# Adapter attention: the second chunk's mask is prepared two steps sooner

## The chip, the cores and the metric

The program runs on one core of one Trainium2 chip. The metric is the device time of one execution in microseconds (us), as the median of three. The engines named below are TensorE (PE, the matrix unit; PEld is its weight load), VectorE (DVE), ScalarE (ACT), GpSimd (POOL) and SyncE (SP), which here only issues DMAs.

## The reference, cut to what matters

A post-norm decoder layer over 16 sequences of 128 rows, width 256. Three blocks follow one another: self attention (16 heads of 16), adapter attention (32 heads of 8, with a mask, plus a second attention over a context tensor), and a block with attention of 16 heads of 128 and a mixture of four experts.

```python
x = _layernorm(x + _L0_attn_ref(x, L0_attn_Wqkv, ...), axis=-1)
x = _layernorm(x + _L0_xattn_ref(x, mask_Bx1xSxS_fk0, ctx_2048, L0_xattn_Wq, ...), axis=-1)
x = _layernorm(x + _L0_ffn_ref(x, ...), axis=-1)

# _L0_xattn_ref, the block that the change touches
scores = jnp.einsum('bhqd,bhkd->bhqk', q, k) * inv_sqrt_d
scores = scores + attention_mask
scores = jnp.maximum(scores, jnp.finfo(scores.dtype).min)
w = jax.nn.softmax(scores.astype(jnp.float32), axis=-1)
attn_output = jnp.einsum('bhqk,bhkd->bhqd', w, v)
# plus tanh(gate) * softmax(q a_k) a_v with keys and values from ctx_2048
```

The mask is a float tensor of [16, 1, 128, 128], one 128x128 block for each sequence.

## The kernel before

The first two attention blocks (A, the self attention, and B, the adapter attention) share one software pipeline. It is a loop over steps s from -20 to 361, and every engine runs its own copy of the loop with its own list of what it does at each step. Semaphores tie the engines together; the order of the instructions on each engine is fixed by the step tables alone. All of A's units (4 heads of one sequence, n = 0 to 63) and B's units (n = 64 to 319, in pairs from step 64) go through three passes: `pass1` (scores, whose row maxima the DVE takes), `pass2` (the same scores turned, with the maxima subtracted by extra rows of the stack), `pv` (the product with the values). For B, `pass2` of a unit comes 26 steps after `pass1`, and `pv` 30 steps after it.

The sequences of B come in chunks of two: chunk c = 8 is the first of B, c = 9 the second, whose units start at step 96 (unit 96). A chunk of B has 32 steps. `bg0(c)` is the step to which the background work of a chunk is tied: 44 for c = 8, 64 for c = 9, then 32 more for each. `places` makes tables {step: (chunk, k)} from offsets to `bg0`: `xts` (turning of the inputs), `projs` (projections, with `evacs`, `ropes`, `sums`, `splits`, `parts` and `stacked` derived from them), `masked` and `vals` (values).

How a chunk's mask becomes usable. The mask [128, 2, 128] lies in `MK`. The mask has to be added inside PE by a matmul with bf16 operands, so it is split into three bf16 parts:

- `clamp` (DVE, line 800), at the step in `clamps`
- `mask_part` and `mask_rest` in turn, at the steps in `mask_parts`: ACT line 1042, POOL line 1175, ACT line 1045, POOL line 1177. They write the tile `B_MQ`.
- `mask_out` (SP, DMA `Bmask<-B_MQ`), at `masks_out`, and two steps later `mask_rows` (SP, DMA `B_MP<-Bmask`), which reads it back in another layout. `mask1` on PE (line 562, matmuls `bank<-B_MP,B_pick`) adds it to the scores of `pass1`; the chunk's first unit needs it, at step 96 for c = 9.
- `masks` (PE, line 536) turns the f32 mask at `masked`, ACT (line 1005) copies it out of PSUM into `MT` one step later. `mask_parts_turned` (PE, line 545) turns the three parts at `mask_turns`, ACT (line 1011) copies them into `B_MTQ`, and SP sends them out and back at `masks_t_out` (`Bmask<-B_MTQ`, `B_MTP<-Bmask`) for `pass2`, which is 26 steps later.

Of one step, PE does `pv`, the mask products, `pass2` and `pass1` first. From step 87 on values and the small turns follow, then `transpose_in`, projections, `masks` and `mask_parts_turned`; before step 87 the values and small turns stand behind these. Each small PE product gets its PSUM bank from the table `home`, which deals banks 5, 6, 7 in rotation up to step 85 and banks 6, 7 from step 86 in the order of the steps; `turn` on PE waits until the bank's user before it has been read.

What SP does in these steps, in this order within a step: load of the mask (`load_mask`), `shift` (rows `B_nmT` that carry the maxima into the stack), `stack_in` (six DMAs `stk<-Bdrq`, `stk<-Bdrk` or `stk<-Bdra` each, from DRAM into the stack of q, k or adapter k), `mask_out`, `mask_rows`, `mask_t_out`, `mask_t_rows`, `parts_out` (two DMAs `Bdrk<-PB` and so on). All run through one queue on SP, in order: a DMA that waits holds up every one behind it. `shift(17)`, at step 101, feeds `pass2` of units 80 and 81 at step 106.

Of the kernel before, what the change touches and what calls it, by code (L numbers as in the profile page):

```python
# [43 lines left out]
def program(nc, I, out):  # L44
# [204 lines left out]
    def bg0(c):  # L249
        return 8 * c - AHEAD if c < 9 else NA + 32 * (c - 9)  # L250

    def places(A, B8, B9, B):

        return {max(bg0(c) + r, -AHEAD): (c, k) for c in range(16)
                for k, r in enumerate(A if c < 8 else B8 if c == 8 else B9 if c == 9 else B)}

    xts = places((-1,), (-2, -4), (-2, 4), (-8, 8))
    projs = places((2, 6), (2, 6, 10), (0, 10, 13), (-4, 9, 13))
    masked = places((), (11,), (23,), (18,))
    clamps = {s - (6 if c < 10 else 7): c for s, (c, _) in masked.items()}  # L260
    mask_parts = [{s + k: c for s, c in clamps.items()} for k in (1, 2, 3, 4)]
    masks_out = {s + 5: c for s, c in clamps.items()}
# [2258 lines left out]
```

## Time and profile before

| | us |
|---|---|
| median of three runs | 1181.89 (1181.88 to 1181.89) |
| profiled execution, its own time | 1185.99 |
| its span | 1184.2 |
| PE busy | 1116.1 (94%) |
| PE weight load busy | 921.1 (78%) |
| DVE busy | 954.0 (81%) |
| ACT busy | 667.3 (56%) |
| POOL busy | 660.2 (56%) |

The profiled execution is 4.1 us longer than the median, and its span 1.8 us shorter than its own time. The step tables place the second chunk's mask work between about 209 and 231 us of the span. Blocks A and B end near 550 us; the rest is the third block, which the change does not touch.

How to read the rows: a timeline row gives start, duration, engine, line, operation, `out<-in`, shape and count; in brackets is the idle time of the engine before it, and what ended it. Several instructions of one form that follow each other stand in one row. `SPq` is a DMA being issued, not the transfer. PEclk 1.00 is TensorE's clock of 2.4 GHz, 0.50 is 1.2 GHz.

### The profile page before, as it was taken

How to read it: one execution, taken by the hardware profiler on the slowest of the kernel's cores; microseconds unless marked ns; L12 is line 12 of the kernel's file. 1: busy time of each engine (PE TensorE's matmuls, PEld its weight loads, DVE VectorE, ACT ScalarE, POOL GpSimd, SP SyncE). 2: the span in 40 equal slices, each digit the busy share in tenths (PEclk: the TensorE clock that was granted, in tenths of full speed). 3: DMA queues.
4: the chain of work that ended last, by engine and by line, in shares of the span. 5: the costliest groups of instructions: out<-in, count | busy, mean ns of one | idle time of the engine just before them, and what ended most of it. 6: DMA issues, size and time to landing. Idle time of an engine off the chain costs nothing.

```text
span 1184.2 us, 30629 instructions
## 1 busy us (share of the span) xinstructions
PE 1116.1 (94%) x11732; PEld 921.1 (78%) x11732; DVE 954.0 (81%) x2219; ACT 667.3 (56%) x1703; POOL 660.2 (56%) x714
## 2 busy tenths in 40 slices
PE   6899999899999999888999999999999999999997
PEld 5667665566666766556899899999999899988887
DVE  6758886877888878867788888888898888878977
ACT  5466564577777777664555544444444444558663
POOL 4457564654545556264778554544544455737665
PEclk9889999989999999989999999999999999999999
DMA  5975544344444444402121000000000100101111
GB/s 162 211 183 131 130 122 110 99 122 120 120 135 135 117 126 119 121 22 86 58 72 55 2 1 1 1 1 1 1 1 1 37 2 1 37 19 36 37 37 36
DMA packets 107490, 83.05 MB, mean 70 GB/s; under 512 B 74171, under 2 KB 95803, under 8 KB 107345
## 3 DMA queue, kind: packets, MB, share of 16 engines
q1 hardware_dynamic: 107345, 81.10, 25.0%
q8 instruction: 93, 1.52, 0.5%
q14 instruction: 52, 0.43, 0.1%
HBM read 57.02 MB, written 23.07 MB: 68 GB/s over the span
## 4 chain that ended last, share of the span: by engine, by line
PE 55%; DVE 14%; issue 6%; POOL 4%; ACT 2%; SPq 1%; DMA 1%; POOLq 0%; DVEq 0%; ACTq 0%
PE bank L1637 5%; PE bank L1638 5%; PE bank L1639 5%; PE bank L1693 4%; PE bank L1666 4%; PE bank L665 3%; PE bank L643 3%; PE bank L562 3%; PE bank L1653 2%; PE bank L1708 2%; PE bank L1706 2%; PE bank L1707 2%; DVE B_nr L808 2%; PE bank L1654 2%; PE bank L1655 2%
## 5 line engine op out<-in xcount | busy, mean ns | idle before, releaser
L1941 POOL TENSOR_TENSOR C_QK<-C_t1b,C_t2b 128x512 f32<-128x512 f32 x128 | 168.7, 1318 | 227.4 <-DVE C_t2b L1780 226.8
L1777 DVE SCALAR_TENSOR_TENSOR C_t1b<-bank,C_bcol,C_tabs 64x512 f32<-64x512 f32 x256 | 192.1, 750 | 38.6 <-PE bank L1639 34.5
L1067 ACT ACTIVATE PT<-bank 128x512 f32<-128x512 f32 x224 | 130.0, 596 | 98.5 <-PE bank L643 96.7
L808 DVE TENSOR_REDUCE B_nr<-bank 128x4 f32<-128x512 f32 x256 | 164.2, 683 | 25.4 <-PE bank L604 25.1
L1637 PE MATMUL bank<-C_XTh,C_Wh 128*128 128x512 f32 x256 | 112.4, 439 | 5.7 <-DVE C_XTl L1626 1.9
L1873 ACT ACTIVATE C_P<-bank,C_nm 128x128 f32<-128x128 f32 x256 | 90.5, 366 | 34.1 <-DVE C_nm L1790 32.4
L1892 ACT ACTIVATE C_V<-bank 128x512 f32<-128x512 f32 x64 | 38.0, 596 | 124.1 <-PE bank L1655 122.6
L1638 PE MATMUL bank<-C_XTl,C_Wh 128*128 128x512 f32 x256 | 101.6, 397 | 0.0
L1639 PE MATMUL bank<-C_XTh,C_Wl 128*128 128x512 f32 x256 | 101.2, 395 | 0.0
L665 PE MATMUL bank<-PT,vpool 128*32 128x128 f32 x2048 | 97.6, 287 | 2.0 <-ACT OTf L1077 2.0
L1780 DVE SCALAR_TENSOR_TENSOR C_t2b<-bank,C_bcol,C_tabs 128x512 f32<-128x512 f32 x128 | 96.1, 751 | 1.8
L643 PEld LDWEIGHTS bank<-stk 54*128 54x128 bf16 (+1 forms) x1280 | 49.4, 96 | 50.6 <-issue 37.3
L1881 ACT ACTIVATE C_OTh<-bank,C_bcol 128x512 fp32r<-128x512 f32 x64 | 44.1, 689 | 73.7 <-PE bank L1693 73.1
L604 PE MATMUL bank<-stk 48*128 48x128 bf16 (+1 forms) x1280 | 77.0, 220 | 6.2 <-DVE B_nr L808 5.9
L643 PE MATMUL bank<-stk 54*128 54x128 bf16 (+1 forms) x1280 | 77.2, 222 | 3.9 <-DMA stk<-A_nmT 3.5
L1801 DVE SCALAR_TENSOR_TENSOR C_OTl<-bank,C_bcol,C_OTh 128x512 fp32r<-128x512 f32 x64 | 47.9, 748 | 38.8 <-ACT C_OTh L1881 38.7
L1653 PE MATMUL bank<-C_Wh,C_XTh 128*128 128x256 f32 x256 | 72.5, 283 | 1.6 <-DVE C_t2b L1780 1.3
L1706 PE MATMUL bank<-C_Wh,C_OTh 128*128 128x256 f32 x256 | 71.9, 281 | 0.4 <-DVE C_OTl L1801 0.4
L1654 PE MATMUL bank<-C_Wl,C_XTh 128*128 128x256 f32 x256 | 71.9, 281 | 0.0
L1655 PE MATMUL bank<-C_Wh,C_XTl 128*128 128x256 f32 x256 | 71.9, 281 | 0.0
L1708 PE MATMUL bank<-C_Wh,C_OTl 128*128 128x256 f32 x256 | 71.7, 280 | 0.0
L1707 PE MATMUL bank<-C_Wl,C_OTh 128*128 128x256 f32 x256 | 71.6, 280 | 0.0
(271 smaller groups left out, 3495.0 us busy)
## 6 DMA issues: line engine op xcount, KB each, us to landing
Adrq<-PB SPq DMA_DIRECT2D x16, 192.0 KB, 2.9
Adrk<-PB SPq DMA_DIRECT2D x16, 192.0 KB, 3.1
stk<-Adrq SPq DMA_DIRECT2D x16, 192.0 KB
stk<-Adrk SPq DMA_DIRECT2D x16, 192.0 KB
Bdrq<-PB SPq DMA_DIRECT2D x16, 192.0 KB, 3.0
stk<-Bdrq SPq DMA_DIRECT2D x32, 96.0 KB
Bdrk<-PB SPq DMA_DIRECT2D x16, 192.0 KB, 2.8
stk<-Bdrk SPq DMA_DIRECT2D x32, 96.0 KB
```

The costliest lines, as they stand in the source:

```text
L643: m = e.matmul(bank2(n)[:, j * 128:j * 128 + 128], (AS if kd else KS[L])[i3][rows, h, :], QS[L][i3][rows, h, :], start=alone, stop=alone o ...
L665: m = e.matmul(o[32 * j:32 * j + 32, c3 * 128:c3 * 128 + 128], vp[:, h, :], pt_of(n)[:, j * 128:j * 128 + 128], start=first or not L, stop ...
L808: e.tensor_reduce(dst, bank[n % 2][:, :].rearrange("p (a b) -> p a b", a=4), AX.X, ALU.max, negate=True).then_inc(sem("m_dve"), 1)
L1067: e.activation(pt_of(n)[:, :], bank2(n)[:, :], ACT.Exp).then_inc(sem("e_act"), 1)
L1637: e.matmul(o[:, :], CWh[hp][:, cs], XCh[0][:, t, :], start=t == 0, stop=False)
L1638: e.matmul(o[:, :], CWh[hp][:, cs], XCl[0][:, t, :], start=False, stop=False)
L1639: m = e.matmul(o[:, :], CWl[hp][:, cs], XCh[0][:, t, :], start=False, stop=t == 1)
L1653: e.matmul(ob, XCh[0][:, t, xs], CWh[hp][:, cs], start=t == 0, stop=False)
L1654: e.matmul(ob, XCh[0][:, t, xs], CWl[hp][:, cs], start=False, stop=False)
L1777: e.scalar_tensor_tensor(out=v4(t1b[kq][lo:lo + 64, :]), in0=v4(o[hi:hi + 64, :]), scalar=bc[hi:hi + 64, :], in1=tabsC[hi:hi + 64, 2 * kq ...
L1780: e.scalar_tensor_tensor(out=v4(t2b[kq][:, :]), in0=v4(o[:, :]), scalar=bc, in1=tabsC[:, 2 * kq, :].unsqueeze(1).to_broadcast([128, 4, 128 ...
L1941: e.tensor_tensor(QK[v % 3][:, kq, :], t1b[kq][:, :], t2b[kq][:, :], ALU.add).then_inc(sem("rc_pool"), 1)
```

## The change

One offset in the table of the masked chunks changes: for c = 9 it is 21 instead of 23.

```diff
     xts = places((-1,), (-2, -4), (-2, 4), (-8, 8))
     projs = places((2, 6), (2, 6, 10), (0, 10, 13), (-4, 9, 13))
-    masked = places((), (11,), (23,), (18,))
+    masked = places((), (11,), (21,), (18,))
     clamps = {s - (6 if c < 10 else 7): c for s, (c, _) in masked.items()}
     mask_parts = [{s + k: c for s, c in clamps.items()} for k in (1, 2, 3, 4)]
     masks_out = {s + 5: c for s, c in clamps.items()}
     mask_turns = {s + (1 if c < 9 else 4 if c < 10 else 14): c for s, (c, _) in masked.items()}
```

What follows for chunk 9: `clamp` at step 79 (was 81), the parts at 80, 81, 82, 83 (were 82 to 85), `mask_out` at 84 (86), `mask_rows` at 86 (88), `masks` at 85 (87), `mask_parts_turned` at 89 (91). `masks_t_out` hangs on `bg0` and stays at 94, with the transfer back at 96. Since `home` deals the banks in the order of the steps, two keys change places: the turned mask `("mt", 9)` has bank 5 (was 6), and the value product `("v", 9, 0, 1)` of step 86 has bank 6 (was 7). No other chunk moves, and no instruction is added or removed.

On POOL, steps 81 to 85, where the two subtractions of the mask parts (lines 1175, 1177) stand among those of the projections' parts (lines 461 and 464, tiles `y` and `PB`) and the layer norm's power (line 776):

```order
-L461 TENSOR_TENSOR y<-y,PB 128x512
-L1175 TENSOR_TENSOR B_MR<-stk,B_MQ 128x256
-L464 TENSOR_TENSOR PB<-y,PB 128x512
-L776 TENSOR_TENSOR rstd<-ve,mhalf 128x1
-L461 TENSOR_TENSOR y<-ab,PB 128x512
-L1177 TENSOR_TENSOR B_MQ<-B_MR,B_MQ 128x256
+L1175 TENSOR_TENSOR B_MR<-stk,B_MQ 128x256
+L461 TENSOR_TENSOR y<-y,PB 128x512
+L1177 TENSOR_TENSOR B_MQ<-B_MR,B_MQ 128x256
+L464 TENSOR_TENSOR PB<-y,PB 128x512
+L776 TENSOR_TENSOR rstd<-ve,mhalf 128x1
+L461 TENSOR_TENSOR y<-ab,PB 128x512
```

Line 1177 now stands ahead of the first line 464 and of the power of line 776, and both mask subtractions come before the second line 461.

On PE, steps 89 and 90: the value product of step 89 (lines 496 to 498), then the turning of the mask parts (line 545), then the mask products and pass 2 of step 90:

```order
 L497 MATMUL bank6<-B_Wl,XTh1 128x256
 L498 MATMUL bank6<-B_Wh,XTl1 128x256
+L545 MATMUL bank7<-identb,B_MQ 128x128 [waits xt_dve,mq_pool]
+L545 MATMUL bank7<-identb,B_MQ 128x128 x5
 L562 MATMUL bank2<-B_MTP0,B_pick 32x512 [waits mtp_in]
 L562 MATMUL bank2<-B_MTP0,B_pick 32x512 x3
```

The six turns stood 18 matmuls later, after pass 1 of step 90. They wait for `xt_dve`, the DVE's read (line 794) of bank 7, which holds the inputs turned at step 88. On ACT, line 1011, which reads them, moves with them: it now stands ahead of the copies of the value product and of the exponentials (lines 1067 and 1060) of step 90.

On SP, between the stacks of q and k of chunk 9 (`Bmask` is the DRAM buffer of the mask, `B_MP1` the tile of its rows):

```order
 L1242 DMA stk<-Bdrq1 16x1x2048
 L1242 DMA stk<-Bdrq1 8x2048
-L1242 DMA Bmask0<-B_MQ 128x768 [waits mp_in,mq_pool]
+L1242 DMA B_MP1<-Bmask0 96x4x256 [waits mp_in]
 L1242 DMA stk<-Bdrk1 24x1x2048 [waits parts_k1]
 L1242 DMA stk<-Bdrk1 16x1x2048
```

The write out stands before the two `Bdrk<-PB` now, and the transfer back takes the place that the write out had; it stood behind the six DMAs of the k stack and the two of `Bdra<-PB`.

## Rows read from the trace of the kernel before

**Rows 1.** Timeline of PE, 218 to 247 us: start, us, engine, line, operation
```profile
218.57 0.38 PE L496 MATMUL bank<-B_Wh,XTh 128*128 128x256 f32 x1 [0.84 <-DVE z L872]
...
220.72 0.40 PE L604 MATMUL bank<-stk 48*128 48x128 bf16 x8 [0.96 <-DVE B_nr L808]
...
223.24 0.51 PE L545 MATMUL bank<-identb,B_MQ 128*128 128x128 bf16 x6
...
225.24 0.40 PE L604 MATMUL bank<-stk 48*128 48x128 bf16 x8 [0.75 <-DVE B_nr L808]
...
229.08 0.40 PE L562 MATMUL bank<-B_MTP,B_pick 96*32 96x512 bf16 x4
231.03 0.62 PE L562 MATMUL bank<-B_MP,B_pick 96*32 96x512 bf16 x8 [1.55 <-DMA B_MP<-Bmask]
...
246.82 0.40 PE L643 MATMUL bank<-stk 54*128 54x128 bf16 x8
```

**Rows 2.** Timeline of PE, the same two places 32 steps later (chunk 10)
```profile
274.17 0.67 PE L562 MATMUL bank<-B_MP,B_pick 96*32 96x512 bf16 x8
...
287.18 0.40 PE L643 MATMUL bank<-stk 54*128 54x128 bf16 x8
```

**Rows 3.** Stretches: us, busy (instructions) of PE, PEld, DVE, ACT, POOL, PEclk, DMA share, GB/s
```profile
231.00:233.00 2.00, 1.75 (x40) 0.98 (x40) 0.95 (x2) 0.82 (x2) 1.86 (x4) 1.00 0.35 94
233.00:243.00 10.00, 9.61 (x112) 5.79 (x113) 4.73 (x8) 5.33 (x11) 2.48 (x3) 0.50 0.32 101
243.00:253.00 10.00, 10.00 (x176) 7.81 (x175) 8.07 (x16) 6.25 (x18) 3.73 (x5) 0.99 0.47 132
```

**Rows 4.** Timeline of SP, the DMAs as they are issued
```profile
216.20 0.98 SPq L1242 DMA_DIRECT2D Bdrk<-PB  x2
...
221.90 0.36 SPq L1242 DMA_DIRECT2D Bmask<-B_MQ  x1
...
227.21 0.58 SPq L1242 DMA_DIRECT2D B_MP<-Bmask  x1
229.72 4.10 SPq L1242 DMA_DIRECT2D stk<-Bdra  x6
...
237.76 0.36 SPq L1242 DMA_DIRECT2D Bmask<-B_MTQ  x1
...
241.52 0.33 SPq L1242 DMA_DIRECT2D B_MTP<-Bmask  x1
241.89 1.62 SPq L1242 DMA_DIRECT2D stk<-B_nmT  x2
```

**Rows 5.** Timeline of POOL, steps 81 to 85
```profile
213.00 1.27 POOL L461 TENSOR_TENSOR y<-y,PB 128x512 f32<-128x512 f32 x1
214.23 0.67 POOL L1175 TENSOR_TENSOR B_MR<-stk,B_MQ 128x256 f32<-128x256 f32 x1
215.01 1.16 POOL L464 TENSOR_TENSOR PB<-y,PB 128x512 bf16<-128x512 f32 x1
216.13 0.55 POOL L776 TENSOR_TENSOR rstd<-ve,mhalf 128x1 f32<-128x1 f32 x1
216.64 1.16 POOL L461 TENSOR_TENSOR y<-ab,PB 128x512 f32<-128x512 f32 x1
217.76 0.72 POOL L1177 TENSOR_TENSOR B_MQ<-B_MR,B_MQ 128x256 bf16<-128x256 f32 x1
```

**Rows 6.** Timeline of DVE: two layer-norm writes, and the read of bank 7
```profile
211.78 0.41 DVE L781 TENSOR_SCALAR X<-z,mv,rstd 128x256 f32<-128x256 f32 x1
...
216.76 1.20 DVE L781 TENSOR_SCALAR X<-z,mv,rstd 128x256 f32<-128x256 f32 x1
...
222.38 0.69 DVE L794 TENSOR_TENSOR XTl<-bank,XTh 128x512 fp32r<-128x512 f32 x1
```

**Rows 7.** Timeline of ACT: the copy of the turned mask parts
```profile
224.47 0.79 ACT L1011 ACTIVATE B_MTQ<-bank 128x768 bf16<-128x768 bf16 x1
```

**Rows 8.** Timeline of SP: a DMA of the maxima's rows, block A
```profile
193.72 0.79 SPq L1242 DMA_DIRECT2D stk<-A_nmT  x1
```

**Rows 9.** Timeline of PE: the pass 2 that waits for it
```profile
196.02 0.40 PE L643 MATMUL bank<-stk 99*128 99x128 bf16 x4 [0.46 <-DMA stk<-A_nmT]
```

## The prediction

> **What bounds the kernel now.** I read the page's engine shares first (PE 94% busy, the next, DVE, 81%), then the list of waits for the one DMA that PE waits for in block B, then the timelines of PE, SP, POOL, ACT and DVE around it, and last the stretches with the granted clock. PE's timeline shows the place: PE ends the mask product of pass 2 at about 229.5 us, and the mask product of chunk 9's first unit starts at 231.03, after 1.55 us of idleness that the DMA `B_MP<-Bmask` ended [rows 1]. It is the only such wait in block B. SP issued that DMA at 227.21, behind the k stack and `Bdra<-PB` [rows 4]; it is late because SP's queue is full, not because the mask parts are late.
>
> The stretches show something larger behind it: from 233 to 243 us TensorE runs at 0.50, the 1.2 GHz level, with 9.61 of 10 us busy, and is back at 0.99 to 1.00 after that [rows 3]. What the wait and the slow clock cost together can be read against chunk 10, which has the same work in the same order. From its first mask product to pass 2 ten steps on it takes 287.18 - 274.17 = 13.01 us [rows 2]; chunk 9 takes 246.82 - 231.03 = 15.79 us [rows 1]. So the slow clock costs 2.8 us, and the wait 1.55: if PE went through at 2.4 GHz without the wait, 4.35 us would be free at 246.82. That is the upper end of what the change can bring (0.37% of 1181.89).
>
> **SP, the part that the change is about.** The write out of the parts now needs POOL line 1177 to have ended. In the new order POOL, from 213.03 on, does line 1175 (0.67), line 461 (about 1.25), line 1177 (0.70) and only then line 464, which starts at about 215.65 instead of 215.01 [rows 5]. Line 1177 ends at 215.65, SP has by then the two DMAs `stk<-B_nmT` to issue until about 216.1, the write out goes at 216.1 and costs no queue time that was not idle. `Bdrk<-PB` waits for line 464, so it goes at 216.84 instead of 216.20 [rows 4]: +0.64. Then the six q DMAs, then `B_MP<-Bmask` where the write out stood (0.36 to 0.58 against 0.36), then the six of the k stack. `B_MP<-Bmask` is issued at about 222.5 instead of 227.21, 4.7 us sooner, and even the 3.8 us that it took to land before (227.21 to 231.03) would have it there at 226.3, 3 us before PE asks. So the wait of 1.55 goes. I take it as certain, as far as this DMA goes; the k stack, which is asked for 0.9 us later, is issued 0.6 us later than before and was not waited for at all.
>
> **SP, what comes behind.** All that SP does from `Bdra<-PB` on is a chain of issues and of waits for landings: the six `stk<-Bdra` at 229.72, which waited for `Bdra<-PB` to land, six of the k stack, the turned mask out at 237.76, its transfer back at 241.52 after it had landed, and then `stk<-B_nmT` from 241.89 to 243.51 [rows 4]. None of these had to wait for PE. Leaving `B_MP<-Bmask` out behind `Bdra<-PB` saves nothing, since SP waits for the landing there anyway. So `stk<-B_nmT`, whose two DMAs carry the maxima for pass 2 of units 80 and 81, keeps the +0.6: from 242.5. A transfer of this kind that PE waited for landed at about 196.0, 2.3 us after its issue began at 193.72 [rows 8, 9]. The second of the two is issued from 242.7 before and 243.3 after the change; it lands at about 245.0 before and 245.6 after. PE used it at 246.82 without a wait [rows 1], so 1.8 us of slack are there, and 1.2 us are left of it after the change. **This is the term that sets my forecast**: pass 2 at step 106 can't start before 245.6, so PE can gain 246.82 - 245.6 = 1.2 us, however early it comes. Bounds: it can't land before its own issue ends, at 243.51 + 0.6 = 244.1, which would leave 2.7 us free; at the 3.8 us that the turned mask's write took (237.76 to 241.52) it lands at 247.1 and nothing is. I take the 2.3 us, the row of the same kind of transfer.
>
> **PE, before step 96.** Four things move.
>
> 1. The clamp (0.28 us) leaves the DVE where it had just waited for ACT and enters at about 209.4 beside a POOL instruction. At most 0.5 us, hidden behind the next point.
> 2. The power of the layer norm (line 776) on POOL waits for line 464: 216.8 instead of 216.13, +0.65. The DVE's write of X (line 781) waits for it and started at 216.76; it took 1.20 us, against 0.41 for the same work at 211.78, and ended as POOL's line 461 (216.64 to 217.80) did [rows 5, 6]. I take it that it will again end with line 461, which now runs to 218.5: +0.65 for the DVE, so that pass 1 of step 88, which waited 0.96 us for the DVE at 220.72, starts at 221.35 [rows 1].
> 3. The value product of step 86 has another bank, and its wait of 0.84 us for the DVE's `z` goes [rows 1]. It buys nothing: pass 1 of step 88, next but one, waits for the maxima anyway. The idleness before it grows to about 2.4 us in one piece (218.8 to 221.3).
> 4. The turning of the mask parts now stands before pass 2 of step 90 and waits for the DVE's read of bank 7, which ended at 223.07 [rows 6] and now ends at 223.7. Before, PE came to it at 223.24, with pass 2 and pass 1 behind it [rows 1]. Now pass 2 of step 90 starts at about 224.3. On ACT the copy (0.79 us) [rows 7] stands ahead of the value copies and of step 90's exponential, which ends at 226.3 and holds the mask product of step 92; the maxima of step 90 end at 226.9. So pass 1 of step 92, at 225.24 before [rows 1], comes at 227.0: +1.75.
>
> With +1.75 PE comes to the mask product of unit 96 at 229.5 + 1.75 = 231.2 or, without the 0.25 us of small gaps that close up, 231.0. It was 231.03. **The wait is not taken away but exchanged** for waits of the DVE and of ACT six to eight steps earlier. Bounds for this part: 0 (if ACT and DVE keep up) to +2.3 us.
>
> **The Trainium skill on point 2.** The row shows 1.20 us against 0.41, and an end within 0.2 us of POOL's. SBUF — State Buffer, "Who interferes with whom", says that DVE and GpSimd share a pair of ports under an exclusive lock, held for the whole instruction, and that the loser is blocked. By that rule the DVE write ends with POOL's line 461 (+0.65), as I have it; without it the write would take 0.41 us from 217.4 and end at 217.8, before its old end, and PE would come to unit 96 some 0.65 us sooner. In neither case does the forecast change, as PE then only waits longer at step 106.
>
> **The sum.** If the clock stays at 2.4 GHz after 231.0, PE is at pass 2 of step 106 at 231.0 + 13.01 = 244.0, waits 1.6 us for `stk<-B_nmT`, and starts at 245.6: -1.2 us. If TensorE runs slowly again in the same place, it is there at 231.0 + 15.8 = 246.8, with no wait: 0. After that, all engines go on in the same order and nothing in the rest changes, so what stands at step 106 stands at the end. Profiled execution: span 1184.2 - 1.2 = 1183.0, own time 1184.8; the median lies 4.1 us under it, so 1181.89 - 1.2 = 1180.7 us.
>
> **The rivals.**
>
> - *Nothing gained.* The idle pieces before step 96 are larger than before (2.4, 0.9 and 1.1 us against 0.84, 0.96 and 0.75), and idle pieces precede the fall of the clock here: the 1.55 us at 229.5 stand 2 us before it [rows 1, 3]. If the slow stretch of about 10 us comes anyway, the time is 1181.9 (+0.2 or -0.4). For it: the idle pieces. Against it: 0.84 and 0.96 us within 3 us of one another left the clock at 1.00 before.
> - *The whole 4.35 us.* PE comes early because ACT and DVE keep up, the clock stays up, and `stk<-B_nmT` lands before 243: 1177.5. Against it stands that SP issues the transfer at 242 or later, whatever PE does; only an earlier landing of `Bdra<-PB` or of the turned mask would shift it. More than half of it, 1179.2, with the shortest landing above.
> - *Slower.* The mechanism is the clock at step 106. The new wait there, 1.6 us as large as the one at 229.5, brings the same fall of the clock, but now in a stretch in which PE is busy 10.00 of 10 us [rows 3], so that ten slow us cost up to 5.0 instead of 2.8: -1.2 + 5.0 = +3.8, so 1185.7; if the clock is back after a third of that, +0.5. It decides when the wait at step 106 exceeds about 1.5 us, thus if PE comes there before 244.1. A wait of 0.96 did not do it, so in between all is open.
> - *The change does not do what it says*: the transfer would be as late as before. The order on SP excludes it.
>
> **How the numbers follow.** Forecast, held at step 106 (-1.2, with or without a short slow stretch: -1.8 to +0.6): 0.50. Nothing gained: 0.20. Slower by a long slow stretch behind the new wait: 0.15, of which a fifth stays under +0.2%. Half or all of the 4.35: 0.15, of which a tenth stays within 0.2%. A measurement of this kernel tells about 0.2%, 2.4 us, from no change, so faster is under 1179.5 and slower over 1184.3. Faster 0.14, same 0.74, slower 0.12. The range that leaves a tenth on each side: 1179.0 to 1184.4.
>
> **What would show it.** In the profile after: no wait of PE for `B_MP<-Bmask`; that DMA issued at about 222.5, `stk<-B_nmT` at 242.5 and not before 242; a wait of PE for `stk<-B_nmT` at step 106 of 1 to 2 us (none if the clock is low from 233 on); line 545 on PE waiting for the DVE's line 794; the mask product of unit 96 at 231.0. I am wrong if PE reaches that product by 229.5, if `stk<-B_nmT` is issued before 241.5, or if the clock falls for 10 us at another place than 233.

## The result: 1186.3 us against 1182.2, a ratio of 1.0025 [1.0013, 1.0037]

| | before | changed |
|---|---|---|
| median, first comparison | 1182.19 (15 runs, 1178.04 to 1188.22) | 1186.28 (15 runs: 14 from 1181.82 to 1188.17, and one of 1352.83) |
| profiled execution, own time | 1185.99 | 1185.30 |
| its span | 1184.2 | 1183.5 |

The run of 1352.83 us, at a mean granted clock of 0.75, is a slow one and is left out of every comparison. Ratio and interval are those of the record; the quotient of the two medians is larger, 1.0035, and that of the two means 1.0027.

On a second occasion the ratio was 1.0009 [0.9994, 1.0024]. Over all runs on record together the changed kernel has a mean of 1185.54 us (29 runs) and the kernel before 1183.30 us (119 runs): 2.2 us or 0.19% slower, with a standard error of 0.4 us. The forecast was 1180.7, its range 1179.0 to 1184.4. The three runs shown before (1181.88 to 1181.89) hid that single runs of the kernel before lie up to 11 us apart (1178.04 to 1189.51).

The two profiled executions differ by 0.7 us, and in the other direction. So their comparison shows what changed, but not what it costs; for that I needed more profiles of both kernels (below).

PE in the changed kernel (a timeline; start, us, engine, line, in brackets the idle time before), against [rows 1]:

```profile
219.65 0.40 PE L604 MATMUL bank<-stk 48*128 48x128 bf16 x8 [1.98 <-DVE B_nr L808]
...
222.14 0.80 PE L545 MATMUL bank<-identb,B_MQ 128*128 128x128 bf16 x6 [0.79 <-DVE XTl L794]
...
224.86 0.62 PE L562 MATMUL bank<-B_MTP,B_pick 96*32 96x512 bf16 x4 [0.40 <-ACT PT L1067]
...
226.19 0.61 PE L604 MATMUL bank<-stk 48*128 48x128 bf16 x8 [0.17 <-DVE B_nr L808]
...
231.94 0.40 PE L562 MATMUL bank<-B_MP,B_pick 96*32 96x512 bf16 x4 [0.33 <-DVE B_nr L808]
...
245.28 0.40 PE L643 MATMUL bank<-stk 54*128 54x128 bf16 x8
```

The wait for `B_MP<-Bmask` is gone (231.94), and the waits that the prediction put in its place are there: 1.98 us before step 88, 0.79 before the turning, 0.40 behind ACT. To compare times I use a mark ahead of all that moves: PE's row of line 685 that ends an idle time of 0.31 us by ACT's `ab` (L977), at step 80. It starts at 208.92 before and at 207.41 in the changed kernel. From it, the mask product of unit 96 stands at 22.11 before and 24.53 now (+2.4), and pass 2 of step 106 (the last row) at 37.90 and 37.87: no change between these two profiles.

The stretches (columns as in [rows 3]) show where TensorE was slow:

```profile
218.00:222.30 4.30, 1.86 (x20) 1.61 (x21) 3.96 (x8) 0.94 (x5) 2.29 (x8) 0.98 0.42 132
222.30:229.00 6.70, 6.13 (x56) 4.36 (x55) 3.86 (x6) 3.69 (x10) 0.00 (x0) 0.50 0.49 119
229.00:232.00 3.00, 2.67 (x64) 1.67 (x62) 1.40 (x3) 1.89 (x4) 1.81 (x3) 1.00 0.28 75
232.00:243.00 11.00, 9.38 (x185) 5.66 (x187) 6.98 (x13) 6.79 (x17) 5.41 (x8) 1.00 0.38 110
```

The 1.2 GHz level (0.50) stands from 222.1 to 229, directly behind the new idle pieces, and no more at 233 to 243. The row ahead of it shows PE busy for 1.86 us of 4.30.

SP's queue in the changed kernel, against [rows 4]:

```profile
212.77 1.62 SPq L1242 DMA_DIRECT2D stk<-B_nmT  x2
214.50 0.39 SPq L1242 DMA_DIRECT2D Bmask<-B_MQ  x1
215.13 1.05 SPq L1242 DMA_DIRECT2D Bdrk<-PB  x2
...
220.18 0.33 SPq L1242 DMA_DIRECT2D B_MP<-Bmask  x1
...
228.45 3.82 SPq L1242 DMA_DIRECT2D stk<-Bdra  x6
...
236.52 0.36 SPq L1242 DMA_DIRECT2D Bmask<-B_MTQ  x1
...
238.66 0.33 SPq L1242 DMA_DIRECT2D B_MTP<-Bmask  x1
...
240.13 1.62 SPq L1242 DMA_DIRECT2D stk<-B_nmT  x2
```

The transfer back is issued 12.77 us behind the mark, 5.5 us sooner than before (18.29). The turned mask took 2.1 us from its write out (236.52) to the transfer back (238.66), where it had been 3.8 (237.76 to 241.52), so SP was ready for `stk<-B_nmT` at 31.6 behind the mark. It was issued at 32.72, against 32.97 before, since it now waited for ACT's copy of the maxima (what SP waits for from 225 to 245 us; total, times, longest):

```profile
SPq L1242 <- ACT B_nmT L1053: 1.1, 1, 1.1
```

This copy reads a bank that PE fills (line 615), so the issue can depend on PE; the prediction had said that it doesn't.

POOL, against [rows 5], and two rows of the DVE, against [rows 6]:

```profile
211.36 0.67 POOL L1175 TENSOR_TENSOR B_MR<-stk,B_MQ 128x256 f32<-128x256 f32 x1
212.03 1.16 POOL L461 TENSOR_TENSOR y<-y,PB 128x512 f32<-128x512 f32 x1
213.15 0.67 POOL L1177 TENSOR_TENSOR B_MQ<-B_MR,B_MQ 128x256 bf16<-128x256 f32 x1
213.94 1.17 POOL L464 TENSOR_TENSOR PB<-y,PB 128x512 bf16<-128x512 f32 x1
215.06 0.56 POOL L776 TENSOR_TENSOR rstd<-ve,mhalf 128x1 f32<-128x1 f32 x1
215.57 1.16 POOL L461 TENSOR_TENSOR y<-ab,PB 128x512 f32<-128x512 f32 x1
```

```profile
207.87 0.67 DVE L800 TENSOR_SCALAR stk<-stk 128x256 f32<-128x256 f32 x1
...
215.65 1.24 DVE L781 TENSOR_SCALAR X<-z,mv,rstd 128x256 f32<-128x256 f32 x1
```

The power of line 776 comes 0.44 us later by the mark (0.65 was predicted), and the DVE's write of X again took 1.24 us and ended with POOL's line 461, at 216.9 against 216.7. The clamp took 0.67 us instead of 0.28, beside a POOL instruction, and PE's next line 685 now waits 0.48 us for the DVE (L832).

### The profile page after: what moved, and what is told of

Same layout as the page of the kernel before. It is cut to its first block, busy times and chain, and to the rows that moved or that the text cites. A ratio compares the mean times of both kernels' runs of the same rounds, so it can differ in the third digit from the quotient of the medians.

```text
span 1183.5 us, 30629 instructions
## 1 busy us (share of the span) xinstructions
PE 1112.7 (94%) x11732; PEld 918.6 (78%) x11732; DVE 959.1 (81%) x2219; ACT 667.9 (56%) x1703; POOL 661.2 (56%) x714
## 4 chain that ended last, share of the span: by engine, by line
PE 63%; DVE 18%; issue 6%; SPq 4%; POOL 3%; ACT 2%; DMA 2%; DVEq 0%; POOLq 0%; ACTq 0%
PE bank L665 5%; PE bank L1637 5%; PE bank L1638 4%; PE bank L1639 4%; SPq L1242 4%; PE bank L1693 4%; PE bank L1666 4%; PE bank L643 4%; DVE B_nr L808 3%; PE bank L496 3%; PE bank L562 3%; PE bank L604 2%; PE bank L1653 2%; PE bank L1708 2%; PE bank L1706 2%
```

## The experiments

Every kernel is read by two numbers. M is the time from the mark to PE's row of line 685 that ends an idle time of 0.9 us by POOL's `ON` (L1170), at step 114; all that the change moves lies in it. "Slow" is the time at the 1.2 GHz level inside M, from the stretches. Ratios are to the kernel before on the same chip.

**Copies of the kernel before.** Is its first profile typical?

> The kernel before, unchanged, timed against itself, with the clock and span of every run. Theory 1 (clock): its times differ from run to run by about 10 us because TensorE's slow stretches fall differently, so a run's time should rise as its mean granted clock falls, by about 12 us for each 0.01 of clock if the slow stretch is fully paid, and its median is about 1182.2. Rival (the spread comes from DMA or another engine): no relation between time and clock. In its own profile theory 1 expects the 1.55 us wait for B_MP<-Bmask at about 231 us again, with or without the slow stretch behind it.

> The kernel before, a third profile. Theory 1: the stretch from step 80 to step 114 takes 45 to 47 us: 47 if the slow clock falls behind a wait for B_MP<-Bmask, 45 if it falls at 219 or not at all. With no slow clock before 229 us the wait for B_MP is there, 1 to 1.6 us.

> The kernel before, a fourth profile, to see how often the slow clock falls in its stretch from step 80 to step 114: 43.95 us without, 45.2 with 3.4 us of it, 47 with 10 us of it so far, once each. By theory 1 it is at or under 47 us and its mean stays 1 to 2 us under that of the changed kernel (46.9, 48.0, 47.2).

> The kernel before, a fifth profile: 43.9 us from step 80 to step 114 without slow clock, 45.2 with 3.4 us of it, 47 with 10 us of it; 926.9 to 928.3 us behind it if the second theory holds, up to 931 if that part is ruled by chance.

> The kernel before, a sixth profile, expectations as for the fifth. In two of four profiles so far no slow clock fell in the stretch; the mean of the six should stay 1 us or more under that of the changed kernel.

| profile of the kernel before | own time | M | slow |
|---|---|---|---|
| the one of the prediction | 1185.99 | 46.96 | 10.2 (233 to 243) |
| before_again (ratio 1.0003 [0.9989, 1.0017]) | 1183.43 | 45.15 | 3.4 |
| before_look | 1180.42 | 43.95 | 0 |
| before_look2 | 1181.04 | 43.87 | 0 |
| before_look3 | 1179.99 | 43.90 | 0 |
| before_look4 | 1182.68 | 44.80 | 3.4 |

It isn't. PE of before_look3 at the mark, at unit 96, at step 106 and at the end of M:

```profile
207.55 0.44 PE L685 MATMUL bank<-ident,ON 128*128 128x128 f32 x2 [0.31 <-ACT ab L977]
...
229.20 0.61 PE L562 MATMUL bank<-B_MP,B_pick 96*32 96x512 bf16 x8 [1.08 <-DMA B_MP<-Bmask]
...
242.39 0.40 PE L643 MATMUL bank<-stk 54*128 54x128 bf16 x8 [0.15 <-DMA stk<-B_nmT]
...
251.45 0.44 PE L685 MATMUL bank<-ident,ON 128*128 128x128 f32 x2 [0.93 <-POOL ON L1170]
```

Step 106 stands 34.84 us behind the mark, where the prediction's row has 37.90. The wait for the mask is there (1.08), TensorE is not slow behind it, and the wait for `stk<-B_nmT` that I expected of the changed kernel is already in the kernel before. In before_again and before_look4 TensorE is slow from step 88 on, PE comes to unit 96 later, and no wait for the mask is left.

The slow stretches of the whole span, added up from windows of 0.5 us, make 34 us in the first profile and 11 to 24 us in the other five, with own times of 1179.99 to 1183.43. Between 7 and 17 us of that lie ahead of the mark, in every profile of every kernel here.

**Copies of the changed kernel.**

> The changed kernel again, for a second profile and a second interval on another occasion. Theory 1 (the stretch between the turn of block A's last output at step 80 and the one at step 114, 46.9 us in both first profiles, is typical for the changed kernel but at the upper end for the kernel before, whose second profile took 45.2): the stretch takes 46 to 47.5 us again, with TensorE at 1.2 GHz for 3.4 to 7 us in it, and the ratio is 1.002 to 1.003. Rival 2 (it only moves slow stretches elsewhere by chance): the stretch lies anywhere between 44 and 47, the ratio can come out at 1.000.

> The changed kernel, a third profile. Theory 1: 46 to 47.5 us from step 80 to step 114, TensorE at 1.2 GHz from about 219 or 222 on, no wait for B_MP<-Bmask. Rival 2: 44 to 47.

> The changed kernel, a fourth profile. If its cost lies where it was made: 46.5 to 48 us from step 80 to step 114, with TensorE at 1.2 GHz for 3.4 us or more between 218 and 232. If it lies behind that: about 929.3 us from step 114 to the end of the span, as in all three so far, against 926.9 to 928.3 in the kernel before.

> The changed kernel, a fifth profile, expectations as for the fourth: 46.5 to 48 us in the stretch by the first theory, about 929.3 us behind it by the second; 927 to 932 there, as in the other kernels, if only chance rules that part.

| profile of the changed kernel | own time | M | slow |
|---|---|---|---|
| first | 1185.30 | 46.93 | 6.8 |
| after_again (ratio 1.0009 [0.9994, 1.0024]) | 1186.73 | 48.01 | 10.2 |
| after_look | 1186.33 | 47.24 | 3.4 and 3.4 |
| after_look2 | 1187.92 | 48.01 | 10.2 |
| after_look3 | 1187.92 | 48.01 | 10.2 |

One stretch of after_look2:

```profile
222.00:233.00 11.00, 9.64 (x98) 6.68 (x97) 5.17 (x9) 4.95 (x14) 1.48 (x3) 0.54 0.46 117
```

All five profiles of the changed kernel have a slow stretch in M, and it begins between 220.9 and 222.8 us (13.0 to 14.8 behind the mark), behind the idle 1.98 us before step 88. Three of the six of the kernel before have one. The means of M are 47.64 and 44.77: 2.9 us, somewhat more than the 2.2 us between the means of the runs. The rest of the span, in which both kernels have the same instructions in the same order, is 929.2 to 929.5 us in the changed kernel and 926.8 to 928.4 before; the other kernels below, with the same rest, have 926.7 to 931.6.

What lengthens the rest is again slow TensorE, in stretches that begin 289 to 318 us behind the mark: in the changed kernel 10.2 us of it in the first profile and 6.8 in each of the other four, in the kernel before 6.8, 3.4, 6.8, 0, 0 and 6.8. Where nothing is slow there (before_look2, before_look3 and, below, banks_as_before and rows_again), the rest is 926.7 to 926.9 us. One stretch of after_look3 and the same of before_look3:

```profile
524.00:536.00 12.00, 9.22 (x105) 5.84 (x99) 6.35 (x12) 4.63 (x10) 5.36 (x5) 0.72 0.03 8
```

```profile
524.00:536.00 12.00, 11.34 (x202) 7.22 (x193) 9.30 (x17) 8.88 (x17) 3.81 (x4) 1.00 0.29 100
```

banks_as_before has the changed kernel's order but for two banks, so this order doesn't force a slow stretch there. Whether it makes one more frequent I can't tell from five and six profiles.

**rows_one_step: the transfer back alone, from the kernel before.**

```diff
-            if s - 2 in masks_out:
-                mask_rows(masks_out[s - 2])
+            for c in [c for t, c in masks_out.items() if s == t + (1 if c == 9 else 2)]:
+                mask_rows(c)
```

> The kernel before with one thing moved: for chunk 9 the transfer B_MP<-Bmask is issued one step sooner, ahead of the two Bdra<-PB on SP. No other engine's order changes. Theory 1 (the change failed because it exchanged the DMA wait for waits of ACT and DVE before step 96, and the idle pieces bring the clock down): here nothing is exchanged, the wait of 1.55 us goes, B_MP is issued at about 226.2 and lands by 228.9, and the slow stretch from 233 on becomes rarer: 2 to 4 us faster than before. Rival 2 (the DMA wait was harmless, and a shift of any kind only moves slow stretches elsewhere): the same within 1 us.

> rows_one_step again (the kernel before with B_MP<-Bmask one step sooner), for a second interval and profile. Its first ratio was 0.9993 [0.9978, 1.0007]. If taking the wait away without an exchange gains: 0.998 to 0.9995 again, 43.7 us from step 80 to step 114 without a slow stretch, about 45 with one of 3.4 us. If it gains nothing: 0.9995 to 1.0005.

Ratios 0.9993 [0.9978, 1.0007] and, run again, 1.0002 [0.9985, 1.0019]: the 2 to 4 us that I had expected are not there. In the first, M is 43.71, with no slow stretch (46.28 in the second, with 3.4 and 6.8 us slow). Step 106 and SP in the first (two fences, PE and SP):

```profile
241.73 0.40 PE L643 MATMUL bank<-stk 54*128 54x128 bf16 x8 [0.37 <-DMA stk<-B_nmT]
```

```profile
238.04 0.33 SPq L1242 DMA_DIRECT2D B_MTP<-Bmask  x1
238.42 1.62 SPq L1242 DMA_DIRECT2D stk<-B_nmT  x2
```

The mask's wait goes without any of the change's costs, and is worth 0.2 us: 43.71 against 43.9. Unit 96 comes 20.89 us behind the mark instead of 21.65 (before_look3), 0.76 us sooner, but most of that waits at step 106 for `stk<-B_nmT`, which PE uses 3.3 us after the issue of the pair begins. That is the mechanism on which my forecast was built, and it exists; but it binds only where PE is early.

The second profile (rows_again) is slow from 232.1 us on, about where the kernel before was slow in the prediction's profile, though PE waits for no mask (a timeline and a stretch):

```profile
229.14 0.40 PE L562 MATMUL bank<-B_MP,B_pick 96*32 96x512 bf16 x4 [0.33 <-DVE B_nr L808]
...
231.88 0.43 PE L562 MATMUL bank<-B_MP,B_pick 96*32 96x512 bf16 x4 [0.61 <-DVE B_nr L808]
```

```profile
232.00:239.00 7.00, 6.83 (x90) 3.59 (x86) 3.00 (x5) 3.84 (x8) 1.71 (x3) 0.51 0.43 126
```

And before_look and before_look3 have the mask's wait (1.13 and 1.08 us) with nothing slow behind it. So the slow stretch from 233 on can't be put down to that wait, which the prediction named as what stood ahead of it.

**turn_late: the changed kernel, its turning put back to step 91.**

```diff
-    mask_turns = {s + (1 if c < 9 else 4 if c < 10 else 14): c for s, (c, _) in masked.items()}
+    mask_turns = {s + (1 if c < 9 else 6 if c < 10 else 14): c for s, (c, _) in masked.items()}
```

> The changed kernel with the turning of the mask parts (PE line 545, ACT line 1011) put back to step 91; clamp, parts, write out, transfer and banks stay two steps sooner. Theory 1, with the turning as the main term: PE's wait of 0.79 us for the DVE's line 794 and the 0.40 us for ACT's exponential go, pass 1 of step 92 comes about 1 us sooner, and of the 3 us that the change costs 1 to 2 come back: about 1184.5. If POOL's order (line 1177 ahead of 464) is the main term, it stays at 1185 to 1186. Rival 2 expects no relation: anywhere from 1181 to 1187.

Ratio 1.0014 [0.9997, 1.0030], M 44.98 with 3.4 us slow. PE's two long waits left:

```profile
218.19 0.40 PE L604 MATMUL bank<-stk 48*128 48x128 bf16 x8 [1.98 <-DVE B_nr L808]
...
223.99 0.40 PE L604 MATMUL bank<-stk 48*128 48x128 bf16 x8 [0.63 <-DVE B_nr L808]
```

The 0.79 and 0.40 us of the changed kernel are gone, the 1.98 us before step 88 are not, and TensorE is slow from 218 to 222 only. By its time alone it can't be told from the changed kernel nor from the one before.

**banks_as_before: the changed kernel with the two old banks.**

```diff
+    home["mt", 9], home["v", 9, 0, 1] = bank[6], bank[7]
```

> The changed kernel with the two banks that changed places put back (turned mask in bank 6, value product of step 86 in bank 7). PE's idle time before step 88 stays the same in sum but is cut in two pieces by the value product, 0.8 and about 1 us in place of 1.98. Theory 1 with the single long idle piece as what brings the clock down: the slow stretch from 222 us on goes, and the time falls by 1 to 3 us against the changed kernel. If only the sum of idleness counts, or if the cost is in the waits themselves: the same as the changed kernel, 1185.5 to 1186.5.

Ratio 1.0017 [1.0002, 1.0033], M 47.27 with 3.4 and 3.4 us slow. PE:

```profile
216.17 0.39 PE L496 MATMUL bank<-B_Wh,XTh 128*128 128x256 f32 x1 [0.43 <-DVE z L872]
...
218.32 0.40 PE L604 MATMUL bank<-stk 48*128 48x128 bf16 x8 [1.18 <-DVE B_nr L808]
```

The 1.98 us in one piece become 0.43 and 1.18. The slow stretch still comes, and M is as in the changed kernel: in this one profile, cutting the idleness into pieces did not take the slow stretch away.

**after_filled: the changed kernel with PE kept busy in the idle pieces.** Ten products of 128x512, whose result nothing reads, seven at step 87 and three at step 89.

```diff
+        fill = lambda s: [e.matmul(bank[2] ..., identb, causalTb ..., start=True, stop=True) for k in range({87: 7, 89: 3}.get(s, 0))] and None
...
-            if s in mask_turns:
+            if fill(s) or s in mask_turns:
```

> The changed kernel with ten extra matmuls that nobody reads (128x512, bf16, into a PSUM bank that is free then): seven at step 87, where PE waits 1.98 us for the DVE, three at step 89 ahead of line 545, where it waits 0.79 us. Nothing else changes. If the idle pieces bring the clock down and the slow clock is the cost: no slow stretch between 218 and 229, the stretch from step 80 to step 114 falls from 46.9 to about 45 us, and the ratio to the kernel before to about 1.001. If the waits for DVE and ACT themselves are the cost: 46.9 us and 1.0025 stay, or get worse by the 0.2 us that the last filler may delay.

Ratio 1.0009 [0.9993, 1.0025]. M is 45.21, 2.4 us less than the mean of the changed kernel. PE, and one stretch:

```profile
216.49 1.69 PE L706 MATMUL bank<-causalTb,identb 128*128 128x512 bf16 x7
218.61 0.40 PE L604 MATMUL bank<-stk 48*128 48x128 bf16 x8 [0.43 <-DVE B_nr L808]
...
220.16 0.82 PE L706 MATMUL bank<-causalTb,identb 128*128 128x512 bf16 x3
...
223.52 0.40 PE L562 MATMUL bank<-B_MTP,B_pick 96*32 96x512 bf16 x4 [1.03 <-ACT PT L1067]
...
224.42 0.40 PE L604 MATMUL bank<-stk 48*128 48x128 bf16 x8 [0.17 <-DVE B_nr L808]
...
228.98 0.40 PE L562 MATMUL bank<-B_MP,B_pick 96*32 96x512 bf16 x4 [0.33 <-DVE B_nr L808]
```

```profile
216.00:230.00 14.00, 11.71 (x160) 7.36 (x160) 10.52 (x19) 7.04 (x21) 5.59 (x12) 1.00 0.46 123
```

With 2.5 us of useless work in the same places the slow stretch is gone, in this one profile, and M is 2.4 us shorter. The kernel before pays 0.9 us for slow stretches too (44.77 against 43.9), so 1.6 of the 2.9 us between the kernels hang on the clock. The other 1.3 us are still there with nothing slow: 45.21 against 43.9. The wait for ACT (1.03) stays. In the total it doesn't show: the rest of this profile's span is 931.6 us, with slow stretches elsewhere.

**turn_late_filled: turn_late with seven of those products, at step 87.** This is the price of the new order on POOL and DVE alone.

> The changed kernel with the turning of the mask parts back at step 91 and seven extra matmuls that nobody reads at step 87, where PE waits 1.98 us for the DVE. With TensorE at 2.4 GHz throughout, the stretch from step 80 to step 114 took 43.95 us in the kernel before and 45.2 us in the changed kernel with fillers. If the early turning (PE line 545 and ACT line 1011 ahead of step 90's work) is the whole of these 1.3 us: 43.7 to 44.0 us here, as in rows_one_step. If POOL's order holds a part: 44.3 to 44.6. No slow stretch between 216 and 232 us. Ratio to the kernel before: 0.998 to 1.000 by the first, 0.999 to 1.001 by the second.

Ratio 0.9999 [0.9982, 1.0015], M 44.15 with nothing slow, between the two expectations. Unit 96 stands 21.31 us behind the mark, against 20.89 in rows_one_step and 22.59 in after_filled: POOL's order and the DVE hold 0.4 us, the turning 1.3 there and 1.1 at the end of M.

**rows_shift_filled: rows_one_step, four filling products at step 87, and the turned mask's transfer back moved behind `stk<-B_nmT`.** The version that the experiments point to.

```diff
-            if s - 2 in masks_t_out:
-                mask_t_rows(masks_t_out[s - 2])
+            for c in [c for t, c in masks_t_out.items() if s == t + (8 if c == 9 else 2)]:
+                mask_t_rows(c)
```

> A candidate that should beat both. From the kernel before: B_MP<-Bmask for chunk 9 one step sooner (as rows_one_step), the transfer B_MTP<-Bmask six steps later, behind the two stk<-B_nmT of step 101, and four extra matmuls that nobody reads at step 87, where PE waits 0.96 us for the DVE. Expected: no wait for B_MP, none for B_nmT (0.37 us in rows_one_step), no slow stretch from 216 to 245 us in most executions; 43.3 us from step 80 to step 114 against 43.95 to 47 in the kernel before; ratio 0.998 to 0.9995. If slow stretches elsewhere decide the time: ratio anywhere within 0.1% of 1.

Ratio 0.9998 [0.9983, 1.0013]. M is 43.30, as expected and the shortest of all, without the wait at step 106. It is 0.6 us under the kernel before with nothing slow, and by time it can't be told from it. So no version beats the kernel before by its time.

## Why the prediction was wrong

With nothing slow in M, the kernels stand so: before 43.9, rows_one_step 43.71, turn_late_filled 44.15, after_filled 45.21. Each is one profile, before is three (43.87 to 43.95). Their differences price the parts of the change:

| part | us |
|---|---|
| the wait for the mask taken away | -0.2 |
| POOL, clamp and DVE later | +0.4 |
| turning (line 545, line 1011) ahead of step 90 | +1.1 |
| slow TensorE, the remainder to 47.64 - 44.77 | +1.6 |

The prediction had a gain of 1.2 us; the changed kernel is 2.2 us slower in its runs and 2.9 us in M. Taken step by step:

- **SP: right, a little off.** The transfer back was issued 12.8 us behind the mark (13.6 predicted) and the wait for it went. The +0.6 for `stk<-B_nmT` did not come: -0.25. The turned mask landed sooner, and what then held the issue was ACT's copy of the maxima (1.1 us), though the prediction said of this chain that nothing in it waits for PE. "The only such wait in block B" holds for `B_MP<-Bmask`; PE waits once more for a DMA there, 0.29 us for `stk<-B_nmT` at 510.39.
- **The DVE beside POOL: right.** The rows of both kernels (1.20 and 1.24 us, ending within 0.2 us of POOL's line 461) agree with the rule of the Trainium skill, SBUF — State Buffer, "Who interferes with whom". The agreement is not exact: a write held back until POOL's end would end its whole 0.41 us behind it, and it ended 0.16 us behind in both. The power came 0.44 us later instead of 0.65, and so did pass 1 of step 88. I took the later write for harmless, because PE would only wait longer at step 106. But it lengthens the idleness before step 88, which stands ahead of every slow stretch of the changed kernel.
- **The exchange of waits: right in place, order and size while TensorE is fast; the clock was left out.** Pass 1 of step 92 was predicted 1.75 us later, at 18.1 behind the mark. In after_filled, with nothing slow, it is at 18.03. In the changed kernel it is at 18.78, and unit 96, predicted at 22.1, at 24.53, against 22.59 in after_filled. These 1.9 us are the slow stretch from 222.1 on (its mask products take 0.62 us and the six turns 0.80, against 0.40 and 0.49 in after_filled). The sum let TensorE be slow from 233 on or not at all, and had no term for this.
- **"This is the term that sets my forecast": the step that failed.** The term was 246.82 - 245.6 = 1.2 us, held by `stk<-B_nmT`. Its first number is not the kernel's. 246.82 is 37.90 us behind the mark; in before_look3 it is 34.84. I expected the changed kernel there at 245.6, 36.7 us behind the mark; the kernel before is earlier than that in all its other profiles (34.8 to 36.1), in three of them held at `stk<-B_nmT`. It had 0.2 us to gain, not 4.35. The changed order with nothing slow (after_filled) reaches step 106 at 36.16, 1.3 us later than the kernel before, and there the hold by `stk<-B_nmT` is 0.15 us. The forecast lowered a median of runs by what was wrong with one profile: "the median lies 4.1 us under it" was the warning. That profile holds 34 us of slow TensorE in its whole span, the five others 11 to 24, and the 2.8 us of slow clock that I wished to win back were a part of it. How much slow time the three runs shown held is not on record.
- **The rivals.** "Nothing gained" named the cause, larger idle pieces before step 96, and gave it 0.20 and no loss, since it set the same 2.8 us against them on both sides. "Slower" put the fall of the clock at step 106, behind a wait that doesn't come there. "0.84 and 0.96 us within 3 us of one another left the clock at 1.00 before" was true of that profile; before_again, before_look4 and rows_again show 3.4 us of slow clock from step 88 on at the same two pieces. So with these pieces TensorE became slow there in three of eight profiles, and with those of the change (1.98 us, or 0.43 and 1.18) in all seven. The sign "if the clock falls for 10 us at another place than 233" came true: 6.8 us from 222.1 in the first profile, 10.2 us from 221.5 to 222.8 on in three others.
- **The range** (1179.0 to 1184.4) came from three runs within 0.01 us. Each kernel's runs spread with a standard deviation of about 2 us. The mean of all of the changed kernel's runs, 1185.54, lies over the range too.

Open is why the first comparison shows 4.1 us and the second 1.4; the runs' spread covers both. Open too is whether the slow stretches in the rest of the span are more frequent by the change's doing. That idleness brings the slow stretch in M rests on seven profiles with the longer idleness, all slow there, and on after_filled and turn_late_filled, in which filling took it away. In the times of the runs the fillers don't show: 1184.38 us on average against 1184.83 for the changed kernel on the same chip, with a standard error of about 0.9. That turning early alone costs 1.1 us is the difference of these two single profiles.

## What to carry to other kernels

Before a wait is valued, compare the profiled execution with the runs: where it lies above them, find its slow TensorE stretches, and don't count as gain what most runs don't pay. A change that takes one wait from PE and makes several smaller ones closer together can cost more by the clock than by the waits themselves (here 1.6 against 1.3 us). Of work moved earlier, ask what the engine did in the place where it now stands: here the transfer needed to move by one step, and the turning and the subtractions that came along cost 1.5 us.

## What was not expected of the hardware

- A program on one core, with the same instructions each time, varied by 11 us (1178.04 to 1189.51). Over the 104 later runs of the kernel before the time falls by 6.9 us for each 0.01 of mean granted clock, with a correlation of -0.76. I had expected 12 us.
- Two profiles of one kernel had their slow stretches in different places, inside M none at all or up to 10.2 us.
- The same transfer chain, the turned mask out to DRAM and its transfer back, took 3.8 us in one profile (237.76 to 241.52), and 2.1 in another (236.52 to 238.66).
